# Cross-attention on one core: weights normalised before the turn, output produced turned, row statistics on ScalarE

## The reference

```python
xq  = (1 + scale_q)  * layernorm(x_q)  + shift_q      # x_q 16 x 1024 x 512
xkv = (1 + scale_kv) * layernorm(x_kv) + shift_kv     # x_kv 16 x 64 x 512
q = xq @ Wq + bq;   k, v = split(xkv @ Wkv + bkv)
attn = softmax(q k^T / sqrt(32))                      # per head, over 64 keys
out  = x_q + (attn @ v) @ Wp + bp
```

## Time and profile before

| | |
|---|---|
| median of 3 runs | 1211.86 us (1210.32 to 1213.16) |
| the profiled execution | 1211.32 us, its span 1209.5 us |
| granted TensorE clock | 0.992 of full |
| busy PE, PEld | 1180.0 us (98%), 772.5 us (64%) |
| busy DVE, ACT, POOL | 980.4 us (81%), 703.0 us (58%), 706.0 us (58%) |

### The profile page before, as it was taken

One profiled execution on the slowest core, in us unless ns is written; L12 is line 12 of the kernel. 1 busy time (PEld: TensorE's weight loads), 2 busy tenths in 40 slices (PEclk: granted clock), 3 DMA queues, 4 the chain that ended last, 5 costly groups with the idle time before them and its releaser, 6 DMA issues.

```text
span 1209.5 us, 33685 instructions
## 1 busy us (share of the span) xinstructions
PE 1180.0 (98%) x11584; PEld 772.5 (64%) x11584; DVE 980.4 (81%) x2052; ACT 703.0 (58%) x1176; POOL 706.0 (58%) x948
## 2 busy tenths in 40 slices
PE   7799899999999999999999999999999999999997
PEld 2675666666666666666666666666666666666664
DVE  4787888888888888888888888888888888888875
ACT  1466556665656556665656565565656565565653
POOL 1553656657474756666575756666565656656434
PEclk9799999999999999999999999999999999999999
DMA  8110222332223232232323222323223222222222
GB/s 330 62 44 27 88 89 97 89 95 87 98 84 99 86 101 86 96 95 88 95 87 95 87 95 87 101 85 100 87 95 92 90 95 87 95 87 84 65 71 80
DMA packets 59866, 111.93 MB, mean 93 GB/s; under 512 B 6412, under 2 KB 6440, under 8 KB 59832
## 3 DMA queue, kind: packets, MB, share of 16 engines
q1 hardware_dynamic: 41400, 77.92, 21.2%
q10 hardware_dynamic: 18432, 33.56, 7.3%
HBM read 77.90 MB, written 33.55 MB: 92 GB/s over the span
## 4 chain that ended last, share of the span: by engine, by line
issue 46%; POOL 37%; POOLq 2%; DVE 0%; DVEq 0%
POOL xr L414 12%; POOL xh L381 7%; POOL w_lo L420 5%; POOL w_tmp L404 5%; POOL rstd L369 2%; POOL xr L390 2%; POOLq L221 2%; POOL nmv L365 2%; POOL veps L367 2%; POOL cur_sc L399 0%; POOLq L244 0%; POOLq L40 0%; POOLq L399 0%; DVE mv L812 0%; DVE oT_lo L827 0%
## 5 line engine op out<-in xcount | busy, mean ns | idle before, releaser
L553 ACT ACTIVATE q_hi<-ps_q,cur_bq 128x512 f16<-128x512 f32 x126 | 86.6, 687 | 268.0 <-PE ps_q L1113 230.6
L365 POOL TENSOR_TENSOR nmv<-mv,sign 128x2 f32<-128x2 f32 x128 | 27.0, 211 | 352.0 <-DVE mv L812 352.0
L820 DVE TENSOR_TENSOR xT_lo<-ps_t,xT_hi 128x512 f16<-128x512 f32 x128 | 88.5, 692 | 162.4 <-ACT xT_hi L494 162.4
L414 POOL TENSOR_TENSOR xr<-y,xr 128x512 f32<-128x512 f32 x128 | 163.1, 1275 | 46.1 <-ACT y L519 46.1
L390 POOL TENSOR_TENSOR xr<-xr,bp_row 128x512 f32<-128x512 f32 x128 | 163.1, 1274 | 13.1 <-POOL rstd L369 6.9
L876 DVE TENSOR_TENSOR pt_lo<-ps_t,pt_hi 128x512 f16<-128x512 f32 x256 | 164.7, 685 | 3.7 <-ACT pt_hi L543 3.5
L868 DVE TENSOR_TENSOR pr<-ps_s,mx 128x512 f32<-128x512 f32 x256 | 163.7, 681 | 0.0
L856 DVE TENSOR_REDUCE mx<-ps_s 128x8 f32<-128x512 f32 x256 | 158.8, 662 | 0.1
L494 ACT CAST xT_hi<-ps_t 128x512 f16<-128x512 f32 x128 | 75.0, 586 | 142.2 <-PE ps_t L1096 142.0
L584 ACT ACTIVATE pr<-pr,exp_scale 128x1024 f32<-128x1024 f32 x128 | 149.6, 1169 | 6.2 <-DVE pr L868 6.2
L543 ACT CAST pt_hi<-ps_t 128x512 f16<-128x512 f32 x256 | 136.3, 588 | 5.3 <-PE ps_t L1149 5.3
(11 more groups left out here) (160 smaller groups left out, 2323.7 us busy)
## 6 DMA issues: line engine op xcount, KB each, us to landing
x_in<-in_x_dram SPq DMA_DIRECT2D x128, 256.0 KB, 2.6
xr<-in_x_dram SPq DMA_DIRECT2D x128, 256.0 KB, 2.6
out_dram<-xr ACTq DMA_DIRECT2D x128, 256.0 KB, 2.2
raw<-in_L_xcond_Wss_kv_dram SPq DMA_DIRECT2D x4, 512.0 KB, 5.4
cx<-in_ctx_dram SPq DMA_DIRECT2D x1, 2048.0 KB, 12.4
raw<-in_L_xcond_Wss_q_dram SPq DMA_DIRECT2D x4, 512.0 KB, 13.4
raw<-in_L_xcond_Wkv_dram SPq DMA_DIRECT2D x2, 1024.0 KB, 15.7
wq<-in_L_xcond_Wq_dram SPq DMA_DIRECT2D x1, 1024.0 KB, 16.9
```

What stands on the lines that cost most here:

```text
L414: pool.tensor_tensor(xr[:, s, :], y[:, off % 2, :], xr[:, s, :], ALU.add).then_inc(y_ready, 1)
```

## The change

The softmax weights are divided by their row sums before they are turned, no longer the output after the product. The sum of each head's 64 weights is made in two steps: GpSimd adds the two halves of 32 (`half_sums`), VectorE reduces the 32 (`weight_sums`) and takes one reciprocal of 16; then VectorE multiplies `pr` in place by 64 times the reciprocal (`normalise_p`). The values are stored scaled by 1/64 to match. The column of ones is gone. In `weigh` the operands change places: the values of a pair of heads are stationary (128 x 64), the turned probabilities move (128 columns), and two products at a time go to the PSUM partitions 0 to 63 and 64 to 127. The result is already turned, so `turn_o` and the normalising of the output go, and `project_out`, `output`, `add_rows` and the store come one step earlier (3 steps to drain, not 4). The row statistics of x leave VectorE: ScalarE makes a sum (`sum_rows`) and, with the negated mean that GpSimd makes of it (`mean`), a sum of squares (`sum_squares`); in the preparation both stand together as `row_moments`. The steps of all engines are written in a new order. The diff, cut to its core:

```diff
-        vb = sb("vb", [P, 2, PAIRS, 2, VC], F16)
+        vb = sb("vb", [P, 2, PAIRS, 2, DH], F16)
...
-            for i in range(4):
+            for i in range(3):
                 step(B, i)
...
@@ GpSimd @@
+            def mean(b, off):
+                if exists(b, off):
+                    s = off % 2
+                    wait(pool, xh_ready, unit(b, off - 1))
+                    wait(pool, row_stats, 2 * unit(b, off) + 1)
+                    pool.tensor_tensor(neg_mean[:, s:s + 1], row_sum[:, s:s + 1], over_h[:, 0:1], ALU.mult)\
+                        .then_inc(mean_ready, 1)
             def moments(b, off):
-                wait(pool, xh_ready, unit(b, off - 1))
-                wait(pool, ln_mv, upto(b, off))
-                pool.tensor_tensor(nmv[:, s, :], mv[:, s, :], sign[:, :], ALU.mult).then_inc(ln_step, 1)
+                wait(pool, row_stats, 2 * upto(b, off))
+                pool.tensor_tensor(var[:, s:s + 1], row_sq[:, s:s + 1], over_h[:, 1:2], ALU.mult).then_inc(ln_step, 1)
...
+            def half_sums(b, off):
+                if exists(b, off):
+                    wait(pool, exp_done, upto(b, off))
+                    wait(pool, den_done, unit(b, off))
+                    pool.tensor_tensor(half_den[:, :, :], pr[:, off % 2, :, 0:LKV // 2], pr[:, off % 2, :, LKV // 2:LKV],
+                                       ALU.add).then_inc(half_done, 1)
...
             def step(b, i):
+                half_sums(b, i - 1)
+                mean(b, i + 8)
+                add_rows(b, i - 3)
                 moments(b, i + 8)
                 await_moments(b, i + 8)
-                residual(b, i - 3)
+                residual(b, i - 2)
                 normalise(b, i + 8)
-                add_rows(b, i - 4)
                 if 2 <= i <= 5:
                     scaled_wq_lo(b + 1, i - 2)
                 if 1 <= i <= 4:
                     scaled_wq(b + 1, i - 1)
...
@@ ScalarE @@
+            def sum_rows(b, off):
+                if exists(b, off):
+                    wait(act, x_loaded[off % 4], 16 * (2 * b + off // 4 + 1))
+                    wait(act, row_stats, 2 * unit(b, off))
+                    wait(act, mean_ready, unit(b, off - 1))
+                    act.activation(junk[:, :], x_in[:, off % 4, :], ACT.Copy,
+                                   accum_out=row_sum[:, off % 2:off % 2 + 1]).then_inc(row_stats, 1)
+            def sum_squares(b, off):
+                if exists(b, off):
+                    wait(act, mean_ready, upto(b, off))
+                    wait(act, ln_step, 3 * unit(b, off - 1))
+                    wait(act, row_stats, 2 * unit(b, off) + 1)
+                    act.activation(junk[:, :], x_in[:, off % 4, :], ACT.Square, bias=neg_mean[:, off % 2:off % 2 + 1],
+                                   accum_out=row_sq[:, off % 2:off % 2 + 1]).then_inc(row_stats, 1)
...
             def step(b, i):
+                output(b, i - 3)
                 if not (isinstance(b, int) and b == 0 and i == 0):
                     turned_x(b, i + 7)
-                turned_o(b, i - 3)
-                output(b, i - 4)
+                sum_rows(b, i + 8)
+                turned_o(b, i - 2)
...
                 if i == 7:
                     key_blocks(b + 1)
+                sum_squares(b, i + 8)
                 query(b, i + 4)
...
@@ ScalarE, prime @@
                 for t in range(CT + 1):
...
+                    if t == CT:
+                        row_moments(6)
+                        row_moments(7)
+                    if t < 6:
+                        row_moments(t)
...
@@ VectorE @@
+            def weight_sums(b, off):
+                if exists(b, off):
+                    wait(dve, half_done, upto(b, off))
+                    wait(dve, rden_done, unit(b, off))
+                    dve.tensor_reduce(den[:, :], half_den[:, :, :], AX_X, ALU.add).then_inc(den_done, 1)
             def denominators(b, off):
-                    for h in range(2):
-                        wait(dve, pv_mm, 2 * unit(b, off) + h + 1)
-                        dve.reciprocal(rden[:, HALF * h:HALF * (h + 1)], ps_v[:, h, DH:HALF * VC:VC])
+                    wait(dve, den_done, upto(b, off))
+                    wait(dve, norm_done, 2 * unit(b, off))
+                    dve.reciprocal(rden[:, :], den[:, :]).then_inc(rden_done, 1)
-            def normalise_o(b, off):
...
+            def normalise_p(b, off):
+                wait(dve, rden_done, upto(b, off))
                 for h in range(2):
                     hs = slice(HALF * h, HALF * (h + 1))
+                    dve.scalar_tensor_tensor(out=pr[:, off % 2, hs, :], in0=pr[:, off % 2, hs, :], scalar=P_UNIT,
+                                             in1=rden[:, hs].unsqueeze(2).to_broadcast([P, HALF, LKV]),
+                                             op0=ALU.mult, op1=ALU.mult).then_inc(norm_done, 1)
...
             def step(b, i):
                     turned_x(b, i + 7)
-                stats(b, i + 8)
-                await_stats(b, i + 8)
-                turned_o(b, i - 3)
-                mean_var(b, i + 8)
-                denominators(b, i - 2)
+                weight_sums(b, i - 1)
+                turned_o(b, i - 2)
+                denominators(b, i - 1)
+                normalise_p(b, i - 1)
                 score_max(b, i, 0)
                 score_max(b, i, 1)
-                normalise_o(b, i - 2)
                 softmax_shift(b, i)
...
@@ TensorE @@
             def turn_p(b, off):
-                wait(pe, exp_done, upto(b, off))
                 for h in range(2):
+                    wait(pe, norm_done, 2 * unit(b, off) + h + 1)
...
             def weigh(b, off):
-                wait(pe, o_done, 2 * unit(b, off))
-                for h in range(2):
-                    wait(pe, pt_done, 2 * unit(b, off) + h + 1)
-                    for g in range(4):
-                        pair = 4 * h + g
-                        dst = ps_v[:, h, 2 * VC * g:2 * VC * (g + 1)]
-                        for n, (pt, part) in enumerate(((pt_hi, 0), (pt_hi, 1), (pt_lo, 0))):
-                            last = pe.matmul(dst, pt[:, pair, :],
-                                             vb[:, part, 2 * g + h, :, :].rearrange("p h c -> p (h c)"),
-                                             start=(n == 0), stop=(n == 2))
+                wait(pe, oT_done, unit(b, off - 1))
+                wait(pe, pt_done, 2 * upto(b, off))
+                for m in range(KC):
+                    for n, (pt, part) in enumerate(((pt_hi, 0), (pt_hi, 1), (pt_lo, 0))):
+                        for e in range(2):
+                            last = pe.matmul(ps_v[64 * e:64 * (e + 1), off % 2, P * m:P * (m + 1)],
+                                             vb[:, part, 2 * m + e, :, :].rearrange("p h c -> p (h c)"),
+                                             pt[:, 4 * e + m, :], start=(n == 0), stop=(n == 2))
...
             def step(b, i):
                 score(b, i)
                 project(b, i + 4)
                 turn_p(b, i - 1)
-                project_out(b, i - 3)
+                project_out(b, i - 2)
                 turn_x(b, i + 8)
-                turn_o(b, i - 2)
                 weigh(b, i - 1)
```

More of the change, by code:

```diff
@@ L248, in every_step @@
                 step(B - 1, i)
-            for i in range(4):
+            for i in range(3):
                 step(B, i)
-        def bank_o(b, off):
-            return 0 if isinstance(b, int) and PER * b + off >= PER * (B - 1) else 1
         def place(copy, part, t):
@@ L333, in _ @@
             pool.memset(kb[:, :, :, :, :], 0.0).then_inc(bd_ready, 1)
-            pool.memset(vb[:, :, :, :, :], 0.0).then_inc(zeros_ready, 1)
-            pool.wait_ge(zeros_ready, 1)
-            for par in range(2):
-                rows = slice(LKV * par, LKV * (par + 1))
-                pool.memset(vb[rows, 0, :, par, DH:VC], 1.0).then_inc(bd_ready, 1)
-                pool.wait_ge(bd_ready, 2 + par)
+            pool.memset(vb[:, :, :, :, :], 0.0).then_inc(bd_ready, 1)
             pool.wait_ge(consts_ready, 9)
@@ L380, in normalise @@
                     s = off % 2
-                    pool.tensor_scalar(xh[:, s, :], x_in[:, off % 4, :], nmv[:, s, 0:1], rstd[:, s:s + 1],
+                    pool.tensor_scalar(xh[:, s, :], x_in[:, off % 4, :], neg_mean[:, s:s + 1], rstd[:, s:s + 1],
                                        ALU.add, ALU.mult).then_inc(xh_ready, 1)
@@ L447, in layernorm @@
                 def layernorm(f):
+                    mean(0, f)
                     moments(0, f)
@@ L499, in turned_o @@
                     return
-                wait(act, o_turned, upto(b, off))
+                wait(act, pv_mm, upto(b, off))
                 wait(act, out_mm, unit(b, off))
-                act.copy(oT_hi[:, :, :], ps_t[:, bank_o(b, off), :].rearrange("p (k n) -> p k n", k=KC)).then_inc(oT_hi_done, 1)
```

(35 more changed lines are left out.)

100 lines of the change are left out of this document (40 added, 60 removed).

## The result

| | before | after |
|---|---|---|
| median | 1212.51 us (4 runs, 1210.32 to 1213.38) | 1245.79 us (4 runs, 1245.6 to 1246.24) |
| ratio, with 95% interval | | 1.0278 (1.026 to 1.0296) |
| span of the profiled execution | 1209.5 us | 1243.7 us |

The account below looks back on a forecast made before the run. TensorE (98% busy, 8.54 us a step) bounds the kernel before; after, GpSimd decides the heavy steps. 1211.3 + 16.5 for 15 batches + 3 for the ends + 4 for preparation = 1235 us; own range 1222 to 1252, whole range 1180 to 1262.

Parts of the forecast that it names:

- Heavy steps: Steps 3 to 5 of a batch, each after a step with both GpSimd weight operations: forecast 9.3 us each.
- the marks that showed 1.07 and 1.34 for short operations: Profile rows before: GpSimd's small operation took 1.07 (0.2 alone), VectorE's L946 1.34 (otherwise 0.69), read as mutual holding.
- One sign: Sign expected in the trace after: GpSimd's variance operation shows 0.7 to 1.4 us instead of 0.2.
- TensorE's step, 8.08: TensorE's step falls from 8.54 to 8.08 us: turn_o goes (-0.43), weigh takes 0.80 (-0.03).
- Rival B: Much slower: the halves of the new weigh take 1.30, light steps 8.6, batch 70.9, total 1258; chance 0.24.
- VectorE's 7.6: VectorE's work after the change would fill 7.6 of 8.1 us a step; not yet a bound.
- The chain: From one step's first multiplication through exponential, half_sums, reduction and reciprocal to the next step's: 7.75 us.
- the next S comes 9.15 to 9.5 us after this one: Heavy step's length between first multiplications, set by GpSimd's list with small operations held; 9.3 taken.
- Preparation, +4: Preparation before the loop: two statistics units in a row ahead of a query on ScalarE, +4 us.
- +9 bound: Upper end of the forecast for the preparation's loss, given as between 0 and +9 us.
- Ends, +3: Last batch and drain: unprojected steps at 7.75 give +6.7, the four before -1.4, drain about -2.5; together +3.
- A: Faster rival: the multiplications hold GpSimd up by little, steps 3 to 5 take 8.26, batch 65.9, total 1182; chance 0.25.

Follow-up runs that it names:

- e1: Kernel after, with VectorE's two multiplications reading PSUM and SBUF in place of SBUF twice (weights by other numbers): 1214.34 us, ratio 1.0028.
- e8: Kernel after, with GpSimd's residual in the last batch waiting until both multiplications of the tile are done: 1237.64 us, ratio 1.0219.
- e9: Kernel after, with the row statistics back on VectorE and the mean and ScalarE's two passes gone: 1381.69 us, ratio 1.1407.
- e5: Kernel after, with only the preparation's order changed on ScalarE and GpSimd, all work kept: 1234.53 us, ratio 1.0204.

## Why the prediction was right, and where its terms were not

**Right: the direction and its mechanism.** The forecast was 1235, 10.8 under the result, inside its own range. Heavy steps were to be long because the multiplications and GpSimd's small operations hold each other up; e1 takes the hold away and 31 us with it. By the marks that showed 1.07 and 1.34 for short operations, a hold was the right reading. One sign came only in part: L365 shows the forecast's 0.7 in one of the three heavy steps, and in the other two L367 and L369 are the ones held. TensorE's waits of 0.26 and 0.44 fall before `turn_p`, as forecast, but none before `weigh`; the third, 0.23, is for the low part of x.

**TensorE's step, 8.08.** The shortest steps are 8.16, without a gap on TensorE, and `weigh` is 0.79: the forecast's 0.80. The 0.08 over the forecast lies just ahead of it, 0.53 from `turn_x` to `weigh` for 0.44 from `turn_x` to what followed before. Rival B's 1.30 falls, and with it the time by the rule of the Trainium skill (TensorEngine Tiling (Array Packing), Restrictions): if fast loading is off here, its price is not the one that the estimate gave. VectorE's 7.6 measured 7.63 (61.04 busy in the eight steps of 68.8 us).

**The chain.** Its 7.75 measured 7.73, where nothing holds the pair and VectorE waits for GpSimd's half sums; in e8, from the multiplications at 1197.16 to those at 1204.89:

```profile
1203.41 0.69 DVE L862 TENSOR_REDUCE den<-half_den 128x16 f32<-128x512 f32 x1 [1.36 <-POOL half_den L423]
```

The 7.73 of steps 1 to 3 in e1 and e8 is no proof of it: there TensorE works without a gap (busy 7.7 of 7.7 us), and 8.16 less the 0.43 of `turn_x` is the same number.

**Step by step.** Forecast for steps 0 to 7: 8.15, 8.15, 8.2, 9.3, 9.3, 9.3, 8.3, 8.7; measured 8.16, 8.26, 8.39, 8.87, 8.79, 9.05, 8.16, 9.12. The term "the next S comes 9.15 to 9.5 us after this one" was mis-sized: the small operations end 1.97 us (step 4) or 1.7 us (steps 3 and 5) after the multiplications start and not 2.15 to 2.48 after, and the next S comes after 9.05 or 8.8. Each multiplication holds only one of them, the third runs beside the maxima, or has already run ahead of them. Step 7 was 0.4 too short. Together +0.45 a batch for +1.1. The first batch gained 5.5, which the forecast had at 1.1 like the others; no run looks into what makes it so long. Over the 15 batches it is 11.7 for the forecast's 16.5.

**Preparation, +4 for 10.6 (14.6 up to the first mark).** The text put the statistics only at its end, as two units in a row. The trace shows them in TensorE's way from unit to unit, and a lower clock after the longest idle stretch. e9 confirms whose cost it is (14.0 of the 14.6 returned), e5 that it is the order and not the work (12.6 returned). It was outside the +9 bound too, which the long end of the range did not even use (1252 holds +4): the bound counted ScalarE's durations, and not that a unit's chain over three engines sits ahead of the copies others wait for.

**Ends, +3 for 12.0: the worst term.** The forecast took 7.75 for all steps of the last batch. The first four last 7.94 and three times 8.53, the next 9.70, 8.24 and 9.53. It asked what the lock does where the small operations stand behind `add_rows`, and not what stands there when no x is left: e8 returns 7.2 of the 12.0. And it priced the steps without projection at the full clock, though its own 7.75 leaves TensorE idle there. In three of these steps of the kernel after the multiplications come 9.2 to 9.4 us after those of the step before, in place of 8.54; in e8 it is 8.61 twice in place of 7.73. The granted clock is about 0.8 in these steps, and that costs 0.7 to 0.9 us each time: 1.8 of the 4.7 that e8 leaves.

So the total came near partly by luck: two terms were 6.6 and 9.0 too small, and one was 4.8 too large. The rivals: A's condition, tried in e1, gives heavy steps of 8.16 to 8.51, as it said (8.26), but 1214 and not 1182, since step 7 (9.10) and the preparation stay. A's own steps also add up to 66.3 a batch, not to its 65.9, which would be 1188.

## What to carry to other kernels

Before an operation of VectorE gets both inputs from SBUF, list what GpSimd reads at that moment, in each kind of step and at the ends; a late residual (e8) or one operand from PSUM (e1) takes the price away. When work moves to an engine that is half idle, look at where it stands in that engine's order: the same work cost 14.6 us or 2 up to the first mark, and one exchange of two lines 11 us in the loop. And when one bound is removed, read the next wait ahead of the new bound before calling the edit useless: the full reduction was worth nothing until VectorE's 0.41 us of waiting was covered.

## What was not expected of the hardware

- A hold can be passed on: in e9 `residual` stands in the way of the second multiplication, and this one of GpSimd's next operation. An instruction in two parts (128x512 twice) gives the other engine an opening between them, and the pair is 1.29, 2.09 or 2.38 us by who starts first. The hold reaches operations of one element a partition (0.19 and 0.55 us alone, up to 0.74 and 0.89 held).
- 24 loads of 64 columns and 16 bit with two products going to different halves of the PSUM partitions run at 0.03 us each (24 in 0.79 with their matmuls), as fast as the score's loads (0.78).
- On ScalarE a sum taken along with an activation adds a reading of the accumulator of 0.2 us behind it, twice for each unit.
- The lower clock came back at the end, where a chain over the other engines leaves TensorE idle in each step: granted 0.82, 1.00, 0.82, 0.81 in four following steps of the kernel after, and a step with less than the full clock is 0.7 to 0.9 us longer. In the kernel before it is 1.00 there.
